# yq kept as float16 multiples of 2^-24, two operations in every POOL pass, and both halves of w2 rounded on POOL

## What is computed

```python
# x (2,1024,256), cond (2,128)
U = (cond @ W_dec + b_dec).reshape(2, 257, 30)
param = einsum('bik,kj->bij', U, V)
y = einsum('bsd,bde->bse', x, param[:, :-1]) + param[:, -1][:, None]
def quant_act(a):    # per row
    scale = 127 / clip(max(abs(a), -1), 1e-5)
    return clip(round(a * scale), -128, 127) / scale
def quant_weight(w): # per matrix
    s = clip(mean(abs(w)), 1e-5)
    return clip(round(w / s), -1, 1) * s
h = gelu(quant_act(y) @ quant_weight(w1).T)      # 1024 wide
out = x + quant_act(h) @ quant_weight(w2).T
```

## Time and profile before

| | us |
|---|---|
| runs | 68.60, 68.99, 71.72; median 68.99 |
| profiled execution | 68.60 |
| its span | 66.8 |
| TensorE busy | 57.9 (87%), 13.2 of it warming matmuls (L398) |
| VectorE, ScalarE, POOL busy | 45.1, 35.8, 28.5 |

### The profile page before, as it was taken

One profiled execution on the slowest core, in us unless ns is written; L12 is line 12 of the kernel. 1 busy time (PEld: TensorE's weight loads), 2 busy tenths in 40 slices (PEclk: granted clock), 3 DMA queues, 4 the chain that ended last, 5 costly groups with the idle time before them and its releaser, 6 DMA issues.

```text
span 66.8 us, 1289 instructions
## 1 busy us (share of the span) xinstructions
PE 57.9 (87%) x449; PEld 30.0 (45%) x449; DVE 45.1 (67%) x92; ACT 35.8 (54%) x52; POOL 28.5 (43%) x47
## 2 busy tenths in 40 slices
PE   2999999998896799989977959999999999969920
PEld 0325332122332363433513533755849467959800
DVE  2000708565328784899999698599897989996530
ACT  3506006600067297999987644766959393852000
POOL 6400001000000108997939795376493929960000
PEclk9999999999999999999999999999999999999999
DMA  0899999999999999700099959979699969824062
GB/s 0 225 363 417 398 426 418 414 391 386 416 412 427 432 412 427 294 25 0 0 189 59 218 118 194 174 141 182 125 264 181 157 208 309 320 96 157 0 235 79
DMA packets 18342, 16.18 MB, mean 242 GB/s; under 512 B 14752, under 2 KB 15136, under 8 KB 17952
## 3 DMA queue, kind: packets, MB, share of 16 engines
q1 hardware_dynamic: 18192, 15.86, 79.6%
q10 hardware_dynamic: 144, 0.24, 1.5%
HBM read 10.47 MB, written 2.10 MB: 188 GB/s over the span
## 4 chain that ended last, share of the span: by engine, by line
PE 38%; DMA 20%; DVE 15%; SPq 9%; ACT 8%; issue 4%; POOL 2%; DVEq 0%
DMA w_dec_all<-in_w_dec_dram 16%; PE ps_h L463 14%; PE ps_o L483 8%; PE ps_z L483 7%; SPq L249 5%; ACT w_dec_all L607 4%; DMA yq_t<-yq_h 4%; DVE pair_max L713 3%; DVE h_max L731 3%; PE ps_y L435 3%; DVE o_sb L755 3%; SPq L266 2%; PE ps_z L423 2%; POOL hq_h L370 2%; ACT y_q L596 2%
## 5 line engine op out<-in xcount | busy, mean ns | idle before, releaser
L370 POOL TENSOR_SCALAR hq_h<-w_dec_all,pair_rcp 128x1024 f16<-128x1024 f32 x14 | 15.7, 1118 | 7.9 <-DVE pair_rcp L727 7.9
L463 PE MATMUL ps_h<-w_t,yq_t 128*128 128x512 bf16 x64 | 16.0, 380 | 1.2 <-DMA yq_t<-yq_h 0.7
L713 DVE TENSOR_REDUCE pair_max<-w_dec_all 128x2 f32<-128x2048 f32 x7 | 15.9, 2276 | 0.0
L607 ACT ACTIVATE w_dec_all<-ps_h,pair_c 128x1024 f32<-128x1024 f32 x10 | 10.9, 1112 | 6.4 <-PE ps_h L463 6.4
L398 PE MATMUL ps_h<-warm_h 128*128 128x512 bf16 x39 | 13.2, 459 | 1.3 <-POOL warm_h L308 1.3
L463 PEld LDWEIGHTS ps_h<-w_t,yq_t 128*128 128x128 bf16 x64 | 5.5, 98 | 8.6 <-issue 1.3
L483 PE MATMUL ps_o<-w_t,hq_t 128*128 128x256 f16 x64 | 8.3, 273 | 0.6 <-DVE o_sb L755 0.5
L483 PE MATMUL ps_z<-w_t,hq_t 128*128 128x256 f16 x64 | 8.3, 272 | 0.0
L579 ACT ACTIVATE w_abs<-w_sb 128x1024 f32<-128x1024 f32 (+1 forms) x3 | 2.7, 914 | 9.1 <-DMA w_sb<-in_w_tr_dram 9.0
L398 PEld LDWEIGHTS ps_h<-warm_h 128*128 128x128 bf16 x39 | 3.8, 119 | 7.8 <-issue 5.9
L483 PEld LDWEIGHTS ps_o<-w_t,hq_t 128*128 128x128 f16 x64 | 6.0, 98 | 2.6 <-DVE o_sb L755 0.7
(11 more groups left out here) (83 smaller groups left out, 68.8 us busy)
## 6 DMA issues: line engine op xcount, KB each, us to landing
w_sb<-in_w_tr_dram SPq DMA_DIRECT2D x4, 512.0 KB, 8.7
x_sb<-in_x_dram SPq DMA_DIRECT2D x2, 1024.0 KB, 19.0
out_dram<-o_sb SPq DMA_DIRECT2D x7, 256.0 KB, 2.9
w_dec_all<-in_w_dec_dram SPq DMA_DIRECT2D x3, 512.0 KB, 7.5
w_dec_all<-in_w_dec_dram SPq DMA_DIRECT2D x3, 448.0 KB, 8.2
x_t<-in_x_tr_dram SPq DMA_DIRECT2D x1, 1024.0 KB, 16.7
w_dec_all<-in_w_dec_dram SPq DMA_DIRECT2D x1, 576.0 KB, 10.3
x_t<-in_x_tr_dram SPq DMA_DIRECT2D x2, 256.0 KB, 10.9
```

The costliest lines, as they stand in the source:

```text
L370: pool.tensor_scalar(hq_h[n % NB][:, :], h_tile(n), scale, UNIT, ALU.mult, ALU.mult).then_inc(hq_ready, 1)
L463: last = nc.tensor.matmul(ps_h[k][:, half, :], yq_t[:, p, n % 2, c, :], w1_t[:, c, half * HALF:(half + 1) * HALF], start=(c == 0), stop=(c ...
L607: nc.scalar.activation(h_tile(n), ps_h[n % 2][:, :, :].rearrange("p a n -> p (a n)"), ACT.Gelu, scale=c1_of(n)).then_inc(gelu_done, 1)
L713: nc.vector.tensor_reduce(pair_max[:, p, 2:4], h_pair[p % NH], AXX, ALU.max, apply_absolute_value=True).then_inc(pair_max_ready, 1)
```

## The change

- yq is written by ScalarE directly as float16, an integer times 2^-24: the factor 2^-24 goes into the scales (the maximum is multiplied by 1/(127 * 2^-24)), and the constant MAGIC, the low halves and the subtraction of 16384 are gone. y_q, yq_t and w1_t are float16; the transpositions on TensorE use the float16 identity, and the copies behind them are plain int16 copies.
- `narrow_y` and yq_h are gone. The DMA of pairs 4 to 6 reads y_q and waits for yq_ready. ScalarE's quantisation of pairs 6 and 7 waits for the landing of pair 4's and 5's DMA.
- Both halves of w2 are rounded on POOL, with the c1 of pair 2 between them; ScalarE's rounding of w2 is gone. The rounding has a minimum with 1 as second operation; the clip is a maximum with -1 and a multiplication by 1.
- `factor` and s_w are gone: VectorE writes the scale straight into s12, two columns wide. The h quantisations keep two operations on POOL, now the scale and 1.0; the half of the last tile on VectorE has one.

```diff
-MAGIC = 1.5 * 2 ** 23 + OFFSET
...
-        w1_t = sb("w1_t", [P, DC, H], BF16)
+        w1_t = sb("w1_t", [P, DC, H], FP16)
...
-        y_q = [sb(f"y_q{k}", [P, 2, D]) for k in range(2)]
-        yq_h = [sb(f"yq_h{k}", [P, 2, D], BF16) for k in range(2)]
-        yq_t = sb("yq_t", [P, NP, 2, DC, P], BF16)
+        y_q = [sb(f"y_q{k}", [P, 2, D], FP16) for k in range(2)]
+        yq_t = sb("yq_t", [P, NP, 2, DC, P], FP16)
...
             def transpose_yq(p):
-                sp.wait_ge(yqh_ready, p - 3)
...
+                sp.wait_ge(yq_ready, 2 * p + 2)
...
-            pool.tensor_copy(ident_h[:, :], ident[:, :]).then_inc(s_identh, 1)
...
-            def factor(k, ready):
...
-            def narrow_y(p):
...
             def round_w2(n):
+
                 pool.wait_ge(s_s2, 2)
-                pool.tensor_scalar(part_of(w2_r, n), part_of(w2_sb, n), s_rcp[:, 1:2], None, ALU.mult).then_inc(s_w2r[n], 1)
+                pool.tensor_scalar(part_of(w2_r, n), part_of(w2_sb, n), s_rcp[:, 1:2], 1.0, ALU.mult, ALU.min).then_inc(s_w2r[n], 1)
...
-                pool.tensor_scalar(part_of(w2_t, n), part_of(w2_r, n), 1.0, -1.0, ALU.min, ALU.max).then_inc(s_w2q[n], 1)
+                pool.tensor_scalar(part_of(w2_t, n), part_of(w2_r, n), -1.0, 1.0, ALU.max, ALU.mult).then_inc(s_w2q[n], 1)
...
-                pool.tensor_scalar(hq_h[n % NB][:, :], h_tile(n), scale, UNIT, ALU.mult, ALU.mult).then_inc(hq_ready, 1)
-
-            factor(0, s_s1)
+                pool.tensor_scalar(hq_h[n % NB][:, :], h_tile(n), scale, 1.0, ALU.mult, ALU.mult).then_inc(hq_ready, 1)
+
             for p in range(AHEAD - 1):
                 scale_y(p)
+            round_w2(0)
+            scale_y(AHEAD - 1)
             round_w2(1)
-            factor(1, s_s2)
-            scale_y(AHEAD - 1)
...
                 if p >= 6:
-                    act.wait_ge(yqh_ready, p - 5)
+                    act.wait_ge(yqt_landed[p % 2], yqt_count(p - 2))
...
                     nc.scalar.activation(y_q[p % 2][:, i, :], y_of[p][:, i, 0:D], ACT.Copy,
-                                         bias=MAGIC, scale=scale).then_inc(yq_ready, 1)
+                                         scale=scale).then_inc(yq_ready, 1)
...
-            act.wait_ge(s_s2, 2)
-            round_w(w2_r[:, 0:HC // 2, :].rearrange("p t c -> p (t c)"), w2_sb[:, 0:HC // 2, :].rearrange("p t c -> p (t c)"),
-                    s_rcp[:, 1:2], s_w2r[0])
...
-                nc.vector.tensor_scalar(pair_inv[:, p, cols], pair_max[:, p, cols], EPS, 1.0 / QMAX,
+                nc.vector.tensor_scalar(pair_inv[:, p, cols], pair_max[:, p, cols], EPS, 1.0 / (QMAX * UNIT),
...
-            nc.vector.tensor_scalar(hq_h[(NT - 1) % NB][:, 0:HALF], h_tile(NT - 1)[:, 0:HALF], h_rcp[:, NT - 1:NT], UNIT,
-                                    ALU.mult, ALU.mult).then_inc(last_hq[0], 1)
+            nc.vector.tensor_scalar(hq_h[(NT - 1) % NB][:, 0:HALF], h_tile(NT - 1)[:, 0:HALF], h_rcp[:, NT - 1:NT], None,
+                                    ALU.mult).then_inc(last_hq[0], 1)
```

More of the change, by code:

```diff
@@ L13 @@
 P = 128
-OFFSET = 16384.0
-MAGIC = 1.5 * 2 ** 23 + OFFSET
 UNIT = 2.0 ** -24
@@ L136, in adaln_ffn, with blocks @@
         ps_z = pb("ps_z", [P, 512])
[L138 to L144, removed]
+        def blocks(bank, n):
+            return bank[:, 0:n * P // 2].bitcast(FP16).rearrange("p (c q) -> p c q", c=n)
+        yq_flat = [y_q[k][:, :, :].rearrange("p t c -> p (t c)") for k in range(2)]
         ps_u = [ps_y[:, 0, :], ps_y[:, 1, :], ps_h[1][:, 0, :], ps_h[1][:, 1, :], ps_o]
@@ L160, in adaln_ffn @@
         late_bank = {LATE: ps_y, LATE + 1: ps_h[0], LATE + 2: ps_y, LATE + 3: ps_h[1]}
-        ps_hqt = {n: [blocks(late_bank[n][:, half, :], HC // 2, FP16) for half in range(2)] for n in late_bank}
+        ps_hqt = {n: [blocks(late_bank[n][:, half, :], HC // 2) for half in range(2)] for n in late_bank}
         o_of = [(ps_o, ps_z)[n % 2][:, 0:D] for n in range(NT)]
@@ L190, in adaln_ffn @@
         s_s2 = sem("w2_scale_ready")
-        s_s12 = [sem(f"w{k + 1}_factor_ready") for k in range(2)]
         s_w1r = [sem(f"w1_rounded{a}") for a in range(DC)]
@@ L334, in scale_pair @@
                 if p == 0:
-                    pool.wait_ge(s_s12[1], 1)
+                    pool.wait_ge(s_s2, 1)
                 pool.tensor_tensor(pair_c[:, p, cols], pair_inv[:, p, cols], s12[:, cols], ALU.mult).then_inc(pair_c_ready, 1)
-            def narrow_y(p):
[L339 to L344, removed]
             def part_of(w, n):
@@ L389, in _ @@
             pool.wait_ge(hqt_landed[(NT - 1 - NB) % LAG], 16 * ((NT - 1 - NB) // LAG + 1))
-            pool.tensor_scalar(hq_h[(NT - 1) % NB][:, HALF:], h_tile(NT - 1)[:, HALF:], h_rcp[:, NT - 1:NT], UNIT,
+            pool.tensor_scalar(hq_h[(NT - 1) % NB][:, HALF:], h_tile(NT - 1)[:, HALF:], h_rcp[:, NT - 1:NT], 1.0,
                                ALU.mult, ALU.mult).then_inc(last_hq[1], 1)
@@ L443, in transpose_yq @@
                 for c in range(DC * i0, DC * i1):
-                    last = nc.tensor.transpose(ps_yqt[n][:, c - DC * i0, :], yq_low[p % 2][:, c * P:(c + 1) * P], ident_h[:, :])
+                    last = nc.tensor.transpose(ps_yqt[n][:, c - DC * i0, :], yq_flat[p % 2][:, c * P:(c + 1) * P], ident_f[:, :])
                 last.then_inc(yqt_done, 1)
@@ L530, in _ @@
             keep_warm(4)
-            pe.wait_ge(s_identh, 1)
+            pe.wait_ge(s_identf, 1)
             transpose_yq(0)
@@ L667, in scales @@
                 dve.wait_ge(s_wall, k + 1)
-                nc.vector.tensor_scalar(s_w[:, k:k + 1], w_all[:, k:k + 1], 1.0 / (H * D), EPS,
+                nc.vector.tensor_scalar(s12[:, 2 * k:2 * k + 2], w_all[:, k:k + 1].broadcast_to([P, 2]), 1.0 / (H * D), EPS,
                                         ALU.mult, ALU.max).then_inc(ready, 1)
                 dve.wait_ge(ready, 1)
-                nc.vector.reciprocal(s_rcp[:, k:k + 1], s_w[:, k:k + 1]).then_inc(ready, 1)
+                nc.vector.reciprocal(s_rcp[:, k:k + 1], s12[:, 2 * k:2 * k + 1]).then_inc(ready, 1)
             def clip_w(dst, src, ready, done):
@@ L700, in y_scales @@
                 dve.wait_ge(y_max_ready, 2 * p + i1)
-                nc.vector.tensor_scalar(y_inv[:, p, i0:i1], y_max[p][:, i0:i1], EPS, 1.0 / QMAX,
+                nc.vector.tensor_scalar(y_inv[:, p, i0:i1], y_max[p][:, i0:i1], EPS, 1.0 / (QMAX * UNIT),
                                         ALU.max, ALU.mult).then_inc(y_inv_ready, i1 - i0)
@@ L735, in h_scales @@
                 dve.wait_ge(h_max_ready, n - SINGLE + 1)
-                nc.vector.tensor_scalar(h_inv[:, n:n + 1], h_max[:, n:n + 1], EPS, 1.0 / QMAX,
+                nc.vector.tensor_scalar(h_inv[:, n:n + 1], h_max[:, n:n + 1], EPS, 1.0 / (QMAX * UNIT),
                                         ALU.max, ALU.mult).then_inc(h_inv_ready, 1)
```

24 lines of the change are left out of this document (6 added, 18 removed).

## The result

| | before | changed |
|---|---|---|
| median of the runs, us | 69.59 (4) | 77.69 (4; 77.56 to 77.82) |
| ratio | | 1.129, interval 1.123 to 1.136 |
| span of the profiled execution | 66.8 | 75.8 |

The forecast was 68.7 us, range 68.1 to 69.8, with 0.08 on slower by over 2%. The kernel is 13% slower. Every ratio here leaves out the runs that lie over 1.5% above the fastest of the same kernel (of the kernel before, 68.60 and 68.99 remain), which is why 1.129 is not 77.69/69.59.

What follows compares the result with a forecast made beforehand. TensorE's full stretch from 40 us was taken as the bound, its start set by VectorE's second maximum, POOL and SyncE's queue. 68.6 - 0.1 (ScalarE), the rest 0, gave 68.5; forecast between 68.5 and 68.9: 68.7 us, range 68.1 to 69.8.

Steps and rivals of the forecast that it cites:

- What bounds the kernel: Loads until about 17 us; TensorE full from 40 to 55 us, where only the beginning of the stretch can move.
- Part 1: ScalarE: dropping its w2 rounding pass of 1.14 us mostly uncovers a wait; gain taken as 0.1 us.
- Part 2: POOL: two w2 roundings of 1.12 us each, clips 2.04 for both; costs nothing by itself.
- Part 3: POOL: dropping three narrowing passes of 0.62 us gains 0, since SyncE's DMA queue is late; ScalarE's new wait costs 0.
- Part 4: float16 yq, scales and the tail's one-operation pass: taken as 0; the tail could gain 0.3 or lose 0.7 us.
- Rival A: VectorE and POOL share a port: pair_inv waits 0.29 for the clips, second maximum +0.17, slower by 0.2 us; chance 0.30.
- Rival B: POOL's int16 output is slow: each rounding 2.85, first h quantisation 2.23 late, slower by 1 us or more; chance 0.18.

Runs made afterwards that it cites:

- e6: e1 with both w2 roundings ahead of pair 2's c1, and pair 4's transposing DMA ahead of tile 2's in SyncE's queue: 68.99 us, ratio 1.001.
- e9: e6 with pair 5's transposing DMA also issued ahead of tile 4's: 69.03 us, ratio 0.995.
- e1: The changed kernel with POOL's w2 rounding as (mult, mult) and its clip as (min, max): 69.42 us, ratio 1.003.
- e3: The changed kernel with only the clip as (min, max), the rounding staying (mult, min): 72.50 us in its one run.
- e2: The changed kernel with only the rounding as (mult, mult), the clip staying (max, mult): 77.96 us in its one run.
- e7: The kernel before with one edit, the w2 clip on POOL as (max, min) instead of (min, max): 74.35 us in its one run.
- e8: The changed kernel with 64 warming matmuls in TensorE's idle stretch before the first product 2: 78.19 us (2 runs).
- e12: The changed kernel with the same 64 warming matmuls as e8, run again with rounds: 77.81 us, ratio 1.120.
- e14: e2 unchanged, run again: 73.53 us; its four runs 73.27, 73.40, 73.66 and 78.08.
- e4: The kernel before with 18 POOL passes of 1024 columns added behind its last one, surveying pairs of operations and types: 108.49 us.
- e13: e2 with 30 warming matmuls in TensorE's idle stretch before the first product 2: 73.65 us.

## Why the prediction was wrong

**What bounds the kernel.** Right. The stretch behind tile 8's product came late with the POOL passes, and in e6 and e9 it moved with pair 4's landing. The delay passed on as the prediction's own figures have it: tile 0's quantisation 9.0 us late; tile 2's, less the 1.17 that POOL idled before it, 7.9; the issue of pair 4's DMA 8.0 (45.30 against 37.29); tile 8's product 8.1. The stretch was full again, but its first product ran at half clock, and from tile 10 on all is 9.0 us late.

**Part 1, ScalarE.** Right in kind: quantisation of pair 2 at 27.80 after an idle of 0.92 (forecast: 27.74 and 0.85), the second maximum at 31.16 (forecast 31.08). Worth 0.02, where the forecast took 0.1.

**Part 2, POOL, is the step that failed,** twice. For the roundings I took "1.12, the row with the same input and width", and they take 3.71: (mult, min) is a slow pair, slower than the 2.85 that was my upper end. For the clips I did not ask at all. The diff turns (min, max) into (max, mult), and the sum carried on 2.04 "for both" from a row of (min, max); they take 7.24. The row was of the same engine, types and width, and of other operations. The bill, from the passes of the earlier trace rows and those after: roundings 3.69 + 3.67 against 2.82 on POOL before, +4.5; clips +5.2; the factor that is gone -0.2; the idle 0.49 ahead of the first h quantisation used up. Together 9.0, the delay from 31.01 to 40.05. In the start of the first h quantisation e1 gives all of it back, e3 what the clips cost (5.1), e2 what the roundings cost (3.9, with the idle stretch that they had used up), and e7 shows the clips' part alone in the old kernel.

**Part 3, the narrowing pass.** Right: nothing gained, the queue is what is late. The new wait of ScalarE never showed.

**Part 4, formats and scales.** Right: e1 has all of it and lies within 1% of the kernel before.

**Rival A** came true in e1 in its mechanism but not in its price: pair_inv was held until the clips ended, as a longer row and not as a later start, and the second maximum began 0.06 late and not 0.17. In the changed kernel it did not, though POOL was busy at 30.52 (see the last section). The prediction said that no row shows such a small pass while POOL works; the trace before had one, of one column, and it was not held (last section too). **Rival B** named the right place and the wrong cause. Its sum was also too small: it let the passes take 2.85 and left the clips as they were. It put 69.7 where 77.7 was measured. Of the 9.0 us of span, 8.1 are the delay through POOL; 0.9 arise in a stretch at half clock, which neither the forecast nor a rival held. Whether they would be saved at full clock is open: e8 and e12 did not show it.

**The range** was drawn from two explanations of one slow pass, and both left the clip alone. A bound for passes whose pair of operations is not in the trace could have been the slowest pass in it for each of the four: 4 x 2.85, which gives the first h quantisation at 25.31 + 11.4 + 0.2 = 36.9 and, by an estimate from e14 (36.75, 73.66), a time near 74. Even that falls short of 77.7: no row of the trace before held a pass of 3.6 to 3.7.

## What to carry to other kernels

A row prices an instruction only if the operations agree too, and in their order: compare them on both sides of a diff before a duration is carried over, above all where an edit looks like a rewriting of the same arithmetic. On POOL, write a scaling as (mult, mult) with a 1.0 and a clip as (min, max), which were fast here at 1024 columns, and time any other pair by itself before it goes on a path. An engine works its program in order, so a pass with urgent work queued behind it costs its whole length, less what the engine would have idled before that work (here 9.0 us of passes less 1.17), whatever another engine saves by the move.

## What the runs showed that was not expected

- A POOL tensor_scalar pass over 1024 columns has three lengths by its operations, 1.04 to 1.12, 2.77 to 2.85 and 3.62 to 3.71 us, and none by its types (e4).
- Whether POOL holds VectorE's small pair_inv up (128x4) depends on the kind of POOL pass. Fast passes did in all six profiles where one had over 0.2 us left at its start: 0.34 us in e1 and 0.54 to 0.86 in e2, e3, e7, e13 and e14. In these rows of e3 and e2 it ended as POOL's clip (34.94) and h quantisation (38.55) did:

```profile
34.15 0.82 DVE L691 TENSOR_SCALAR pair_inv<-pair_max 128x4 f32<-128x4 f32 x1
```

```profile
37.71 0.86 DVE L691 TENSOR_SCALAR pair_inv<-pair_max 128x4 f32<-128x4 f32 x1
```

  Under slow passes it took 0.17 each time, 21 times in nine profiles: at 30.52, 34.08 and 37.53 in the changed kernel, with POOL busy without a break from 25.3 to 46.
- It depends on VectorE's pass too. h_inv, the same two operations on one column, was never held by a fast POOL pass: 0.15 us in all 15 profiles, with 0.20 to 0.66 us of the POOL pass left. The kernel before, VectorE and POOL:

```profile
56.55 0.15 DVE L736 TENSOR_SCALAR h_inv<-h_max 128x1 f32<-128x1 f32 x1
```

```profile
56.08 1.12 POOL L370 TENSOR_SCALAR hq_h<-w_dec_all,pair_rcp 128x1024 f16<-128x1024 f32 x1
```

  What in the two passes makes the difference no run here isolates. The Trainium skill, SBUF — State Buffer, section Who interferes with whom, has the later of the two fully blocked for the whole instruction, where VectorE's is in a mode that uses both ports. The rows of pair_inv agree with it for fast POOL passes and do not for slow ones; which mode a pass was in no row shows.
- One kernel (e2, e14) has two times 4.4 us apart, 73.5 and 78.0. In the two profiles TensorE works at half clock for about 3 us and for over 12, behind an idle stretch of 3.4 us in both. What decides between them was not found.
